# Convolution stage of a graph kernel: the negation, the adjacency's row sums and the layer statistics at other places in the engines' orders

## The reference, cut to what matters

```python
h = jnp.maximum(_layernorm(x, axis=-1), 0.0)          # per node
# in _L0_gnn_ref, with x = h, mask = adj:
h = _bn(_conv1d(xc, conv1_w, 0), ...); h = relu(h)      # 256 -> 256 channels
h = _bn(_conv1d(h, conv2_w, 8), ...)                    # 17 taps over the nodes
x_conv = relu(h + xc)
s = x @ w_se.T + b_se;  A = jnp.exp(-dist(s)) * mask
msg = relu(x @ w_msg.T + b_msg);  x_nmp = A @ msg
# GRU cell on [x_conv, x_nmp], then layer 1: relu(h @ W1 + (adj @ h) @ W2 + bias)
```

## Time and profile before

| | us |
|---|---|
| median of 3 runs | 1814.0 (1813.97 to 1814.85) |
| profiled execution, its own time | 1816.68 |
| its span (first to last instruction) | 1814.9 |
| PE busy in the span | 1732.8 (95%) |
| DVE busy | 1474.1 (81%) |
| ACT busy | 876.8 (48%) |
| POOL busy | 586.1 (32%) |

### The profile page before, as it was taken

The page is one execution under the profiler, slowest core; times in us unless marked ns, Lnnn a source line. Parts: engine busy times, 40 slices in busy tenths (PEclk is TensorE's granted clock), DMA queues, the critical chain, the costliest instruction groups (busy, mean ns, idle before and its releaser), DMA issues. The chain is left out here.

```text
span 1814.9 us, 36602 instructions
## 1 busy us (share of the span) xinstructions
PE 1732.8 (95%) x12222; PEld 1138.3 (63%) x12222; DVE 1474.1 (81%) x3194; ACT 876.8 (48%) x1617; POOL 586.1 (32%) x744
## 2 busy tenths in 40 slices
PE   3778999999998999999999999999999999999997
PEld 2456777764444666666666666666666666666664
DVE  6888888863336888888889888888888888888886
ACT  4665655554343444444444444444444444444442
POOL 5677677720111222222222222222222222222221
PEclk9899999999999999999999999999999999999999
DMA  6297888758743333433433333334334334334331
GB/s 239 90 347 261 295 296 291 251 194 280 224 172 123 110 94 100 115 94 105 115 97 104 108 100 103 106 100 114 94 100 115 94 100 115 94 105 115 96 106 29
DMA packets 242827, 262.70 MB, mean 145 GB/s; under 512 B 82392, under 2 KB 178639, under 8 KB 242255
## 3 DMA queue, kind: packets, MB, share of 16 engines
q1 hardware_dynamic: 242766, 261.94, 46.4%
HBM read 154.92 MB, written 90.18 MB: 135 GB/s over the span
## 5 line engine op out<-in xcount | busy, mean ns | idle before, releaser
L1562 PE MATMUL ps_rz<-big 128*128 128x512 f16 x2304 | 560.0, 379 | 2.3 <-DVE big L1555 2.3
L1562 PEld LDWEIGHTS ps_rz<-big 128*128 128x128 f16 x2304 | 221.8, 98 | 204.4 <-DVE big L1555 2.6
L1562 PE MATMUL ps_n<-big 128*128 128x256 f16 x2304 | 314.2, 273 | 0.2
L1562 PEld LDWEIGHTS ps_n<-big 128*128 128x128 f16 x2304 | 225.1, 98 | 95.2 <-DVE big L1699 1.2
L1562 PE MATMUL ps_l<-big 128*128 128x512 f16 (+1 forms) x1536 | 273.2, 328 | 8.8 <-DVE big L1801 4.5
L1273 PE MATMUL m_ps<-big 128*128 128x512 f16 (+1 forms) x1152 | 268.7, 375 | 4.5 <-DVE big L1040 3.6
L1730 POOL TENSOR_TENSOR big<-big 128x256 f32<-128x256 f32 x128 | 97.6, 763 | 450.5 <-ACT big L1723 450.5
L1562 PEld LDWEIGHTS ps_l<-big 128*128 128x128 f16 x1536 | 150.4, 98 | 97.9 <-DVE big L1801 5.5
L1562 PE MATMUL ps_b<-big 128*128 128x256 f16 x1536 | 188.6, 272 | 2.1 <-DVE big L1630 2.1
L1273 PEld LDWEIGHTS m_ps<-big 128*128 128x128 f16 x1152 | 112.0, 98 | 106.7 <-DVE big L1040 2.4
L1705 ACT ACTIVATE big<-big,w_scale 128x512 f32<-128x512 f32 x128 | 92.7, 724 | 176.7 <-DVE big L1696 176.7
(11 more groups left out here) (240 smaller groups left out, 2780.6 us busy)
## 6 DMA issues: line engine op xcount, KB each, us to landing
spectra<-ysb SPq DMA_DIRECT2D x96, 256.0 KB, 2.5
big<-spectra SPq DMA_DIRECT2D x64, 384.0 KB, 3.5
xin<-in_x SPq DMA_DIRECT2D x64, 256.0 KB, 4.0
x_normed<-front SPq DMA_DIRECT2D x64, 256.0 KB, 3.0
h_turned<-front SPq DMA_DIRECT2D x64, 256.0 KB, 3.8
big<-h_turned SPq DMA_DIRECT2D x64, 256.0 KB, 2.7
big<-in_adj SPq DMA_DIRECT2D x64, 256.0 KB, 3.4
big<-in_x SPq DMA_DIRECT2D x64, 256.0 KB, 2.8
```

What stands on the lines that cost most here:

```text
L1562: last = pe.matmul(dest, stationary(dl), moving(wl), start=start and n == 0, stop=stop and n == 2, **kw)
```

## The change

Three steps are moved, and one count is named. `negate(q)` stands behind `split_h(q)` on ACT, not at the slot's end. The adjacencies are loaded and summed `ADJ_LATER` = 18 slots later: none in slots 0 to 17, and the last 18 in the first units of the unit loop. The biases, which use their buffers, are loaded at u = 22. `layer_stats(q+2)` stands behind `add_bias(q-1)` on DVE, not at the slot's head. The amount of work is the same.

```diff
+ADJ_LATER = GROUP + 2
...
-                    if q < graphs:
-                        load_adj(q)
+                    if ADJ_LATER <= q < graphs:
+                        load_adj(q - ADJ_LATER)
...
                 def load_biases():
-                    sp.dma_start(bias_se[:, :], a["b_se"].partition_broadcast(P)).then_inc(loaded_se, 16)
...
-                sp.wait_ge(adj_seen, graphs)
-                load_biases()
+                sp.dma_start(bias_se[:, :], a["b_se"].partition_broadcast(P)).then_inc(loaded_se, 16)
                 for u, m in enumerate(range(first - HALF_UNITS, len(MAIN))):
+                    if u < ADJ_LATER:
+                        load_adj(graphs - ADJ_LATER + u)
+                    if u == ADJ_LATER + 4:
+                        sp.wait_ge(adj_seen, graphs)
+                        load_biases()
                     if u < HALF_UNITS:
                         load_filters(u)
...
                     if q < graphs:
                         split_h(q)
+                    if 1 <= q < HALF_UNITS:
+                        negate(q)
...
-                    if 0 <= q - 1 < graphs:
-                        adj_sum(q - 1)
-                    if 1 <= q < HALF_UNITS:
-                        negate(q)
+                    if ADJ_LATER <= q - 1 < graphs:
+                        adj_sum(q - 1 - ADJ_LATER)
...
                     split_y(m)
+                    if 2 <= u < ADJ_LATER + 2:
+                        adj_sum(graphs - ADJ_LATER + u - 2)
...
-                    if q + 2 < graphs:
-                        layer_stats(q + 2)
                     if q < graphs:
                         split_h(q)
...
                     if 0 <= q - 1 < graphs:
                         add_bias(q - 1)
+                    if q + 2 < graphs:
+                        layer_stats(q + 2)
...
-                    if u == 20:
+                    if u == ADJ_LATER + 8:
                         bias_sum()
```

## The result

| | before | changed |
|---|---|---|
| median, 6 runs each (us) | 1814.7 | 1806.8 |
| lowest to highest | 1813.97 to 1815.75 | 1805.98 to 1809.4 |
| profiled execution, its own time | 1816.68 | 1806.16 |

The ratio is 0.9959 with a 95% interval of 0.9949 to 0.9969: 7.9 us less by the medians, 8.0 were forecast. The interval is 5.6 to 9.3 us less, so that the two numbers agree to 0.1 us is luck.

The account below looks back on a forecast made before the run. PE bounds the convolution and unit loop, so only slots 0 to 17 can gain: -4.8 - 2.7 - 1.0 + 0.5 = -8.0 us, median from 1814.0 to 1806.0 us, range 1799.5 to 1812.5.

Parts of the forecast that it names:

- What bounds: Whole kernel: PE full from 165 to 385 us and in the unit loop; gain can come from slots 0 to 17 alone.
- The statistics and POOL's loop: Early slots: statistics fill DVE's 0.62 us wait; the loop through POOL then gives 3.9 us in slots 12 to 17.
- 7.7 us for two slots: Early slots: time from one bias addition through statistics, POOL and PE to the bias addition two slots on.
- The negation: Slots 1 to 11: its 1.05 us fits ACT's 1.35 us idle time, removing DVE's 0.23 us wait before L1018.
- The row sums and the store of `ht`: Slots before 12: adjacencies 18 slots later; the store of `ht` sets slots of 4.35 us, bounds 3.9 and 4.65.
- the 5.06 that I reckoned: Slots before 12: time in us from issue to landing of the `ht` store, down from 5.8.
- my inequality: Early slots: three slot lengths are at least 5.4 + 1.4 + the `ht` store's landing + 1.26 us.
- 0.74 us of landing: Slots before 12: 256 KB less per slot at 355 GB/s lets the `ht` store land this much earlier.
- The start of the units: First unit: PE's 2.20 us wait falls to about 1 us, fewer low-clock matmuls; -1.0 us (0 to -1.7).
- Slots 18 to 65 and the unit loop: Slots 18 to 65 PE-bound, 0; unit loop's start gets 18 loads and sums, 0.5 us stall, +0.5 (0 to +7).
- the cover of 3.8: Unit loop: lag in us that ACT may fall behind before PE waits for DVE's reading of three units before.

Follow-up runs that it names:

- e3: Kernel before with only the row sums and their adjacency loads moved 18 slots later; ratio 0.9977, -4.2 us against the kernel before.
- e5: Changed kernel with the negation back at the slot's end on ACT; ratio 0.9963, -6.7 us against the kernel before.
- e7: Changed kernel with row sums 12 instead of 18 slots later; ratio 0.9966, -6.2 us against the kernel before.
- e8: Changed kernel with a second, unused 256 KB adjacency load in each of the first 18 units; ratio 0.9985, -2.7 us against the kernel before.
- e4: Kernel before with negation and statistics moved, row sums where they were; ratio 1.0001, +0.2 us against the kernel before.
- e1: Kernel before with only the statistics moved behind the bias addition; ratio 1.0000, 0 us against the kernel before.
- e11: Kernel before with negation and statistics moved, row sums not, and SP storing the turned graph first; ratio 0.9977, -4.2 us against the kernel before.
- e2: Kernel before with only the negation moved behind the turned graph's reading; ratio 0.9987, -2.4 us against the kernel before.
- e10: Kernel before with SP storing the turned graph ahead of the store of xhat; ratio 1.0005, +0.9 us against the kernel before.
- e9: Changed kernel with the statistics back at the slot's head; ratio 0.9979, -3.8 us against the kernel before.
- e6: Changed kernel with SP storing the turned graph ahead of the store of xhat and load of x; ratio 0.9939, -11.1 us against the kernel before.
- e12: Changed kernel with SP storing the turned graph first and the negation back at the slot's end; ratio 0.9944, -10.2 us against the kernel before.

## Why the prediction was right, point by point

**What bounds.** Right. The gain lies in slots 0 to 17 and just behind; 165 to 385 us and the unit loop stayed full.

**The statistics and POOL's loop.** Right in size: 7.7 us for two slots was worked out, 7.72 is what the bias additions show (134.04 to 141.76). Terms in it were off and nearly cancelled, which is luck. POOL's first small instruction takes 0.54 us, not 0.20, when it starts while DVE runs the low half of `c` (L1039 at 114.02, L832 at 114.19); and PE's `conv1` follows its turn by 0.49 us, not 0.67, and the turn follows POOL by 0.06, not 0.12. The normalisation itself took 2.42 us, as taken. The GPSIMD Engine Reference of the Trainium skill, Specifications, names contention of GpSimd with such a DVE instruction with two SBUF inputs. The trace agrees for the small instruction (0.54 against 0.20), where I had looked at the long one alone.

**The negation.** That it fits into ACT's idle time was right. That it removes DVE's 0.23 us wait is true only against ACT's loop with the row sum in it: in e3 the row sums' move alone has removed it too. With the statistics moved as well the wait is back when the negation is not moved (0.37 us and more in e5).

**The row sums and the store of `ht`.** Right that this store sets the slots before 12: 4.36 us measured, 4.35 taken. It landed 4.2 us after issue, earlier than the 5.06 that I reckoned, but unevenly: slots of 3.7 to 4.0 stand beside ones of 4.3 to 5.3. With the landing of 4.2 my inequality gives 4.1 us, so 4.36 is a mean of slots that wait and slots that do not, and not the steady length that I worked out. And 43.57 against 43.5 is in part luck, since e7 and e8 took 45.16 and 44.15 for the same instructions. What failed is the step's share of the whole. I priced these loads' removal as 0.74 us of landing. e4 shows that without it the other two edits gain nothing, and e1 that the adjacency's own load is late, behind `store_xhat` in SP's order. That wait was not in my list, because the change removed it. My sentence that the sum on ACT hinders no one once the negation has moved is wrong: in e11, with negation and statistics moved, ACT stands 8.4 us before these sums.

**The start of the units.** Right in kind: -1.0 taken (0 to -1.7), -1.66 in the profile. The reason is only half shown. Of the five kernels with the 2.20 us wait three ran the matmuls behind it at a lower clock (before, e2, e10) and two did not (e3, e9). Of the kernels with under 1 us of wait none did. So the shorter wait removes a chance of loss, not a fixed one.

**Slots 18 to 65 and the unit loop.** 0 and +0.5 taken; in the profile 0.1 us more apart from the cold matmuls, and 0.1 less. The +0.5 was worked out from 355 GB/s. At the 377 that were moved, 1 MB is 2.78 us, a lag of 2.3 us over 12 units by the same sum, and that is inside the cover of 3.8: no stall. e8 shows that the cover ends, but not that it is 3.8. At its 403 GB/s a unit of 1.25 MB is 3.25 us, a lag of 7.9 over 12 units by my estimate, of which 5.1 were lost; and PE began to wait six units later than the sum says. Why the wait came so late is open.

## What to carry to other kernels

Filling an engine's wait with work that was done earlier makes that work late for whom it feeds: follow the chain through every engine and every DMA queued behind it in order, and compare the loops that come out, not the waits. Edits that shorten different loops are worth the step down to the next longest one, so test the combination and each without one part. A store that no one waits for is free where it stands until its producer moves; then its place in the queue may be the cheapest thing to change.

## What the runs showed of the hardware that was not expected

The granted clock is not the same from kernel to kernel behind the same idle time. Behind 2.20 us of wait at the first unit it was 0.67 in the next 3 us in the kernel before, 0.53 in e2 and 0.58 in e10, but 1.00 in e3 and e9; the twelve matmuls took 2.15, 2.81, 2.66, 1.49 and 1.49 us. Behind the 3.01 us wait in the last stage it was 1.00 (1.48 us, changed kernel) or 0.50 (2.74 us, before). In the slot from graph 1 to 2 PE waits 1.96 to 2.50 us in the changed kernel, e5, e6, e7, e8 and e12; four of them ran cold behind it, e5 and e12 did not. One such place is worth 1.3 us and more, and 27 executions of the kernel before lie up to 5.3 us apart: a reason not to read a difference of under 2 us from two profiles.

The DMA engines moved 377 GB/s over 40 us of the changed unit loop and 403 in e8, at shares of 1.01 and 1.04. That is more than the 355 that I had scaled from a share of 0.97, and above the limit of some 358 GB/s in the page DMA: Bandwidth & Descriptors (Specifications) of the Trainium skill; the measurement decides. The same page of the Trainium skill (Bandwidth) gives that figure for both cores of a pair streaming at once, and this kernel runs on one core. The bytes counted here are loads and stores together.
